# Graph network kernel: each octet's adjacency blocks leave in one store of fourteen pieces, and the two DRAM tensors are split by octet instead of by piece

## The chip, the cores and the metric

The kernel runs on one core of a Trainium2 chip. The metric is the device time of one execution in microseconds (us), the median of several runs. Lower is better.

## The reference, cut to what matters

A graph of 12,500 nodes with 96 features and 400,000 edges (sorted by destination) passes through two blocks. The first is an edge network, the second two graph convolutions that share one sparse matrix. Only the data flow matters for this change:

```python
# block 1: edge network
edge_input = concat([h[src], edge_attr])                 # 400000 x 128
messages = gelu(edge_input @ mW1 + mb1) @ mW2 + mb2
gates = sigmoid(gelu(edge_input @ gW1 + gb1) @ gW2 + gb2)
aggregated = segment_sum(messages * gates, dst)          # 12500 x 96
update = gelu(concat([h, aggregated]) @ uW1 + ub1) @ uW2 + ub2
# block 2: two layers, each
norm = dinv[row] * w * dinv[col]
xc = segment_sum(norm[:, None] * (x @ W)[row], col) + b  # the same sparse matrix in both layers
g = sigmoid(x @ Wr + br)
x = relu((1 - g) * x + g * xc)
```

## The kernel before, in words

All engines walk the edges in 196 iterations of 16 tiles (a tile is 128 edges). For each quad of four tiles GpSimd gathers the rows of the source nodes into `hid`, TensorE multiplies the edge attributes (`attr`, the product at L1099), VectorE adds the two (L1662), ScalarE applies the gelu and weighs the message (L1358), and TensorE sums the messages by destination (L1155). That is the edge network.

In 192 of the 196 iterations the engines also prepare the convolutions. About half of the edges (1,536 tiles, the "side" tiles) do not go through gathers later. They are turned into small dense adjacency blocks now: eight side tiles make an octet, one octet per iteration. TensorE builds an octet's blocks in eight parts in PSUM (`build_part`, the matmuls at L1132), and ScalarE copies each part into `blocks[h]` in SBUF (`keep_part`, L1367). `blocks` has two halves, h = 0 and 1, used by octets in turn. A full octet is 128 partitions x 98 blocks x 40 floats, 1,960 KB. SyncE's queue stores it to the DRAM tensors `adjacency` (`store_blocks`, L698). The 98 blocks are 14 pieces of seven blocks, and one piece of one octet is 280 floats, 1,120 bytes, in each partition: the longest run that is contiguous in DRAM, since the octets of a piece lie beside each other there.

The convolutions read the tensor back, once for each layer. In a layer ScalarE's queue walks 16 units of 12 octets. For a unit and a piece one load (`load_piece`, L1459) brings 128 partitions x 12 octets x 280 floats, 1,680 KB, into one of four `ring` buffers. TensorE multiplies the piece with the node table (L1240) and signals `eaten`. A piece may be loaded into a slot once the piece four earlier has been eaten. The first 14 units (seven pairs) run in a hardware loop that also carries work on the gate (`mix`), the last pair in a second one. The other half of the edges goes through gathers on GpSimd and small matmuls (L1227) between the pieces.

The order of everything is written out by hand, engine by engine, with semaphores between. What the change touches:

- `edges` on SyncE, one call per iteration. It waits for the gathers two iterations back and loads `src_ids` (L706). Then it loads `attr[0]` and `attr[1]` (L712), each once TensorE has used up that buffer's last content. The stores of the octet two iterations back are mixed in between.
- `store_blocks` waits (L563, in `wait_apart`) until ScalarE has copied all eight parts, `s_evac`.
- `keep_part` 0 of an octet waits on ScalarE until the store of the octet two earlier, which used the same half of `blocks`, has landed (`s_block_out[h]`).
- `edge_pass` builds the loop over octet pairs for every engine, and `conv_pair` and `conv_unit` on ScalarE the loop over unit pairs.

Of the kernel before, what the change touches and what calls it, by code (L numbers as in the profile page):

```python
# [30 lines left out]
P = 128  # L31
# [75 lines left out]
HALF_PIECES = PIECES // 2  # L107
# [64 lines left out]
def build(nc, io):  # L172
    ctx = contextlib.ExitStack()
    with ctx:
# [24 lines left out]
        adjacency = [dram(f"adjacency{i}", [HALF_PIECES, P, OCTETS, PIECE_Z]) for i in range(2)]  # L199
# [377 lines left out]
        def edge_pass(eng, rounds, iteration, round_end=None, part=None, round_start=None, alone=0, end=None, turns=False):  # L577

            with eng.Fori(0, rounds) as r:
                n0 = eng.snap(r * ITERS)
                o0 = eng.snap(r * OCTETS)
                w0 = eng.snap(r * OCTET_PAIRS)

                def turn(half, h):
                    return ((h, eng.snap(r * (ITERS // 2) + half)),) if turns else ()

                def prepare(c, ahead):
                    done = eng.snap(r * SLICES + c)  # L590
                    if part:
# [5 lines left out]
                def pair(w, final):  # L597
                    for h in range(2):
                        o = eng.snap(w * 2 + h) if not isinstance(w, int) else w * 2 + h
                        last = final and h == 1  # L600
                        it = o + BUILD_FROM
                        iteration(it, n0 + it, False, last, (o, eng.snap(o0 + o), h, eng.snap(w0 + w)),
                                  None if last else (o + 1, eng.snap(o0 + o + 1)), *turn(w + BUILD_FROM // 2, h))
# [12 lines left out]
                if round_end:  # L616
                    round_end(r)
# [35 lines left out]
        def _(sp):  # L653
# [40 lines left out]
            def store_blocks(o, nb, h, i):  # L694
                if i == 0:
                    wait_apart(sp, s_evac, nb * PARTS + (PARTS + EVAC_CREDIT))
                kept = blocks[h][:, :, :].rearrange("p (i c b) z -> p i c (b z)", i=2, c=HALF_PIECES)
                sp.dma_start(adjacency[i][:, :, bass.ds(o, 1), :].rearrange("c p q z -> p c (q z)"),  # L698
                             kept[:, i, :, :]).then_inc(s_block_out[h], 16)

            def edges(it, n, first, last, build, ahead, turn):
# [7 lines left out]
                for b in range(GROUPS_PER_ITER):  # L709
# [22 lines left out]
            def edges_end(r):  # L732
                o0 = sp.snap(r * OCTETS)
                for h in range(2):
                    for i in range(2):
                        store_blocks(OCTETS - 2 + h, o0 + (OCTETS - 2 + h), h, i)
                for h in range(2):
                    wait_apart(sp, s_block_out[h], r * (32 * OCTET_PAIRS) + (32 * OCTET_PAIRS + 32))
# [5 lines left out]
            for h in range(2):  # L744
                sp.sem_inc(s_block_out[h], 32)
            edge_pass(sp, rounds, edges, edges_end, round_start=edges_start, alone=1,
                      part=load_side_edges, end=keep_side_rel, turns=True)
# [547 lines left out]
        def _(act):  # L1295
# [76 lines left out]
            def edges(it, n, first, last, build, ahead):  # L1372
# [4 lines left out]
                for s in range(QUADS_PER_ITER):  # L1377
                    weigh(n, s)
                    if build:
                        keep_part(2 * s, *build[1:])  # L1380
# [8 lines left out]
                    if build:  # L1389
                        keep_part(2 * s + 1, *build[1:])  # L1390
# [54 lines left out]
            for l in range(2):  # L1445

                act.wait_ge(tb[l]["scaled"], 2 * CHUNKS)
                if l == 0:
                    for h in range(2):
                        act.wait_ge(s_block_out[h], rounds * (32 * OCTET_PAIRS) + 32)  # L1450
# [5 lines left out]
                def load_piece(w, i, u, nu, s=cv[l]):  # L1456
# [3 lines left out]
                                  adjacency[i // HALF_PIECES][i % HALF_PIECES, :, bass.ds(u * UNIT_OCTETS, UNIT_OCTETS), :]  # L1460
# [7 lines left out]
                def conv_unit(u, w, u0, h0, mix, more, s=cv[l]):  # L1468
                    nu = act.snap(u0 + u)
                    for i in range(RING, PIECES):  # L1470
                        load_piece(w, i, u, nu)
                        if mix and i in TANH_AFTER:
                            mix_tanh(h0 + (u * 2 + TANH_AFTER.index(i)))
                    if more:
                        for i in range(RING):
                            load_piece(w + 1, i, u + 1, nu + 1)
# [5 lines left out]
                def conv_pair(v, u0, h0, mix, more=True):  # L1482
                    for w in range(2):
                        conv_unit(act.snap(v * 2 + w), w, u0, h0, mix, more or w == 0)

                with act.Fori(0, passes) as p:
# [5 lines left out]
                    for i in range(RING):  # L1492
                        load_piece(0, i, 0, u0)
                    with act.Fori(0, MIX_UNITS // 2) as v:
                        conv_pair(v, u0, h0, True)
                    with act.Fori(UNITS // 2 - 1, UNITS // 2) as v:
                        conv_pair(v, u0, h0, False, False)
# [656 lines left out]
```

## Time and profile before

| | us |
|---|---|
| median of 3 runs | 8839.22 |
| lowest and highest run | 8838.54, 8855.53 |
| span of the profiled execution, core 0 | 10933.0 |
| TensorE busy in the profiled execution | 8192.3 |
| GpSimd busy | 6435.5 |
| VectorE busy | 4899.6 |
| ScalarE busy | 2690.1 |

The profiled execution is one execution, recorded by the hardware profiler. Its own time is taken to be its span, 10933.0 us, since the records show nothing around it. It is 2093.8 us longer than the median of the runs without the profiler, so its durations show proportions and what hides what, not the absolute time. TensorE's granted clock had a mean of 0.838 of full speed over the span. The program falls into setup and node tables (to about 300 us), the edge network (to about 5790 us), the node update (to about 6000 us), and the two convolution layers, each with its combination of the results (to the end).

### The profile page before, as it was taken

To read this page: it belongs to the slowest core of one execution; us is meant where nothing else is said; L and a number is where in the kernel's file an instruction comes from. 1 tells how busy PE (TensorE), PEld (TensorE's weight loads), DVE (VectorE), ACT (ScalarE), POOL (GpSimd) and SP (SyncE) were. 2 spreads that over 40 slices of the span, in tenths; PEclk is the share of its full clock that TensorE was granted. 3 is DMA by queue.
4 is the path that set the end of the run, shared out by engine and by line. 5 is a ranking of instruction groups with operands and counts; after the bars stand their busy time and mean duration, and the time that the engine had idled before them with its cause. 6 is when DMAs were issued, how large, how long until landed. Compare 5 with 4: busy or idle time off the path is not lost. (4 is left out here: it accounts for less than half of the span.)

```text
span 10933.0 us, 150076 instructions
## 1 busy us (share of the span) xinstructions
PE 8192.3 (75%) x42144; PEld 5220.9 (48%) x42144; DVE 4899.6 (45%) x11836; ACT 2690.1 (25%) x6600; POOL 6435.5 (59%) x6424
## 2 busy tenths in 40 slices
PE   4777777777777777777777578887777577887776
PEld 4555555555555555555555233333334333433333
DVE  7666666666666666666667122222222121222222
ACT  3444444444444444444443000000000000000000
POOL 4555555555555555555554666666664666666663
PEclk7888888888888888888887788888887688888887
DMA  4444444444444444444444456666565465666656
GB/s 147 123 138 131 136 132 136 132 135 132 135 133 135 133 135 135 134 135 133 135 132 134 155 207 220 216 218 214 208 212 198 156 215 206 224 217 210 210 207 207
DMA packets 933049, 1818.03 MB, mean 166 GB/s; under 512 B 277359, under 2 KB 745600, under 8 KB 875312
## 3 DMA queue, kind: packets, MB, share of 16 engines
q10 hardware_dynamic: 65600, 773.65, 18.6%
q1 hardware_dynamic: 615456, 578.39, 16.9%
q0 software_dynamic: 251856, 464.10, 14.8%
q8 instruction: 93, 1.52, 0.1%
q14 instruction: 44, 0.36, 0.0%
HBM read 1361.12 MB, written 454.48 MB: 166 GB/s over the span
## 5 line engine op out<-in xcount | busy, mean ns | idle before, releaser
L962 POOL DMA_INDIRECT hid<-src_table,src_ids x3127 | 3136.7, 1003 | 2510.4 <-ACT msg L1358 1590.2
L1240 PE MATMUL bd<-ring,table_sb 128*96 128x480 f32 x6272 | 2941.6, 614 | 513.3 <-issue 511.7
L1240 PEld LDWEIGHTS bd<-ring,table_sb 128*96 128x96 f32 x6272 | 1071.7, 176 | 2131.6 <-issue 2131.1
L1007 POOL DMA_INDIRECT hid<-conv_table,hid x1596 | 1561.9, 979 | 751.1 <-issue 486.2
L1155 PE MATMUL sg<-hot,msg 128*98 128x64 f32 x6272 | 831.1, 286 | 1115.9 <-ACT msg L1358 1105.2
L1132 PE MATMUL bd<-one_hot_dst,one_hot_src 128*128 128x168 bf16 (+1 forms) x10368 | 1277.0, 274 | 253.5 <-issue 252.3
L1007 POOL DMA_INDIRECT feat_in<-conv_table,hid x1056 | 1026.1, 972 | 545.2 <-issue 324.6
L1155 PEld LDWEIGHTS sg<-hot,msg 128*98 128x98 f32 x6272 | 746.8, 199 | 1252.2 <-issue 1180.0
L1972 DVE TENSOR_TENSOR acc<-acc,sg 96x64 f32 x400 | 87.2, 218 | 2450.0 <-remote 1652.7
L1132 PEld LDWEIGHTS bd<-one_hot_dst,one_hot_src 128*128 128x128 bf16 x10368 | 1007.1, 110 | 299.1 <-issue 284.3
L1367 ACT ACTIVATE blocks<-bd 128x480 f32<-128x480 f32 (+1 forms) x1152 | 658.1, 571 | 1704.7 <-PE bd L1132 811.8
L1709 DVE SCALAR_TENSOR_TENSOR one_hot_src<-iota_lo,side_now 128x384 bf16<-128x384 bf16 x1536 | 933.8, 608 | 0.0
L1358 ACT ACTIVATE msg<-hid,msg 128x96 f32<-128x96 f32 x3136 | 909.8, 363 | 52.7 <-DVE msg L1686 45.8
L1099 PE MATMUL pa<-w_attr,attr 128*128 128x384 f32 x1568 | 820.1, 660 | 57.9 <-DVE hid L1662 37.9
L1345 ACT ACTIVATE hid<-hid 128x768 f32<-128x768 f32 x784 | 656.8, 838 | 281.2 <-DVE hid L1662 230.6
L1465 ACT ACTIVATE buf_b<-pa,mix_b_half 96x448 f32<-96x448 f32 x56 | 35.3, 630 | 2768.6 <-remote 1515.8
L1007 POOL DMA_INDIRECT rows_more<-conv_table,hid x528 | 526.9, 998 | 301.6 <-issue 153.6
L1612 DVE TENSOR_TENSOR acc<-acc,sg 98x64 f32 x392 | 87.1, 222 | 1284.5 <-remote 1253.3
L1099 PE MATMUL pb<-w_attr,attr 128*128 128x384 f32 x1568 | 592.3, 501 | 7.8 <-issue 4.6
L1950 DVE TENSOR_TENSOR conv_hot<-iota_now,hid 128x512 f32<-128x512 f32 x134 | 92.6, 691 | 958.9 <-remote 517.0
L1099 PEld LDWEIGHTS pa<-w_attr,attr 128*128 128x128 f32 x1568 | 396.9, 280 | 262.6 <-issue 151.8
L1479 ACT ACTIVATE hid<-bd,side_flag 96x480 f32<-96x480 f32 x32 | 21.0, 657 | 1958.2 <-PE bd L1240 1126.1
(248 smaller groups left out, 10307.8 us busy)
## 6 DMA issues: line engine op xcount, KB each, us to landing
ring<-adjacency ACTq DMA_DIRECT2D x448, 1680.0 KB
adjacency<-blocks SPq DMA_DIRECT2D x384, 980.0 KB
attr<-in_attr SPq DMA_DIRECT2D x392, 128.0 KB
hid<-src_table,src_ids POOLq DMA_INDIRECT x3127
hid<-conv_table,hid POOLq DMA_INDIRECT x1596
feat_in<-conv_table,hid POOLq DMA_INDIRECT x1056
conv_table<-table_sb SPq DMA_DIRECT2D x28, 336.0 KB, 2.4
feat_half<-feat_keep SPq DMA_DIRECT2D x56, 168.0 KB
```

Of the source, the lines that this page charges most:

```text
L962: pool.indirect_dma_start(out=hid[s][:, t, :], out_offset=None, in_=src_rows, in_offset=bass.IndirectOffsetOnAxis(ap=src_ids[h][:, j:j + 1 ...
L1007: pool.indirect_dma_start(out=conv_g[j][slot][:, t, :], out_offset=None, in_=conv_rows[l], in_offset=bass.IndirectOffsetOnAxis(ap=conv_ids ...
L1099: last = nc.tensor.matmul(attr_ps[s % 2][:, 512 * h:512 * h + 2 * H2], attr[s // 2][:, P * (s % 2):P * (s % 2 + 1)], w_attr[:, 2 * H2 * h: ...
L1132: op = nc.tensor.matmul(out[:, :, bass.ds(places[q][t], FAN)], y_s[q][t][:, k, :], z_s[q][t][:, z0:z0 + FAN * m].rearrange("p (b d) -> p b ...
L1155: op = nc.tensor.matmul(sums[s // 2][0:ACC_ROWS, :], msg[s % 2][:, t, :], hot[s % 2][:, t, :], start=(s % 2 == 0 and t == 0), stop=(s % 2 ...
L1240: op = nc.tensor.matmul(side_ps[w].rearrange("r (o z) -> r o z", o=UNIT_OCTETS), table_sb[:, D * k:D * (k + 1)], ring[slot][:, :, OCTET_FA ...
L1345: nc.scalar.activation(flat, flat, ACT.Gelu).then_inc(s_gelu, 1)
L1358: op = nc.scalar.activation(m[:, t, 0:D], hid[s][:, t, 0:D], ACT.Copy, scale=m[:, t, GATE_ROW:GATE_ROW + 1])
L1367: nc.scalar.activation(blocks[h][:, first:first + m, WIDTH * q:WIDTH * (q + 1)], part_bank[i % BANKS][:, 0:WIDTH * m].rearrange("p (b w) - ...
L1709: v.scalar_tensor_tensor(out=y_s[q][t][:, :, :], in0=iota_lo[:, :].unsqueeze(1).to_broadcast([P, 3, P]), scalar=side_now[:, 0, QUAD * q + ...
L1950: v.tensor_tensor(conv_s[j][slot], iota_now[:, :].unsqueeze(1).to_broadcast([P, GROUP, WINDOW]), conv_rel[j][:, cols].unsqueeze(2).to_broa ...
L1972: v.tensor_tensor(window, window, sg[j][0:D, WINDOW * slot:WINDOW * (slot + 1)], ALU.add).then_inc(s["acc"], 1)
```

## The change

Before, each octet left in two stores of seven pieces, into `adjacency[0]` (pieces 0 to 6 of all 192 octets) and `adjacency[1]` (pieces 7 to 13 of all octets). The first came after the load of `attr[0]`, the second after the load of `attr[1]`. Now the two tensors are banks of octets: `adjacency[0]` holds all 14 pieces of octets 0 to 95, `adjacency[1]` those of octets 96 to 191. An octet leaves in one store of 14 pieces, behind both loads of `attr`. The distance between two partitions in DRAM falls from 192 x 1,120 = 215,040 bytes to 96 x 1,120 = 107,520 bytes, and that between two pieces halves too. The bytes, the runs of 1,120 bytes that a store writes, and the runs of 13,440 bytes that a load reads stay as they are.

Because a tensor cannot be chosen by a register, a loop body now belongs to one bank. SyncE's loop over octet pairs is cut in two (at pair 49). The two loops over unit pairs of a layer on ScalarE become four: pairs 0 to 2 in bank 0, pair 3 (which loads bank 0 and, ahead, the first pieces of bank 1), pairs 4 to 6 in bank 1, and pair 7. All other engines keep their code.

```diff
-HALF_PIECES = PIECES // 2
+BANK_OCTETS = OCTETS // 2
+BANK_PAIRS = UNITS // 4
...
-        adjacency = [dram(f"adjacency{i}", [HALF_PIECES, P, OCTETS, PIECE_Z]) for i in range(2)]
+        adjacency = [dram(f"adjacency{i}", [PIECES, P, BANK_OCTETS, PIECE_Z]) for i in range(2)]
...
-                with eng.Fori(alone, OCTET_PAIRS - 1) as w:
-                    pair(w, False)
-                pair(OCTET_PAIRS - 1, True)
+                ends = [alone, *([] if cut is None else [cut]), OCTET_PAIRS - 1]
+                for bank, (begin, stop) in enumerate(zip(ends, ends[1:])):
+                    with eng.Fori(begin, stop) as w:
+                        pair(w, False, bank)
+                pair(OCTET_PAIRS - 1, True, len(ends) - 2)
...
-            def store_blocks(o, nb, h, i):
-                if i == 0:
-                    wait_apart(sp, s_evac, nb * PARTS + (PARTS + EVAC_CREDIT))
-                kept = blocks[h][:, :, :].rearrange("p (i c b) z -> p i c (b z)", i=2, c=HALF_PIECES)
-                sp.dma_start(adjacency[i][:, :, bass.ds(o, 1), :].rearrange("c p q z -> p c (q z)"),
-                             kept[:, i, :, :]).then_inc(s_block_out[h], 16)
+            def store_blocks(o, nb, h, bank):
+                wait_apart(sp, s_evac, nb * PARTS + (PARTS + EVAC_CREDIT))
+                sp.dma_start(adjacency[bank][:, :, bass.ds(o - bank * BANK_OCTETS, 1), :].rearrange("c p q z -> p c (q z)"),
+                             blocks[h][:, :, :].rearrange("p (c b) z -> p c (b z)", c=PIECES)).then_inc(s_block_out[h], 16)
...
                     sp.dma_start(attr[b][:, :], chunk(io["attr"], it * 2 + b)).then_inc(s_attr[b], 16)
-                    if build:
-                        o, nb, h, _ = build
-                        if not (isinstance(o, int) and o < 2):
-                            store_blocks(o - 2, nb - 2, h, b)
+                if build:
+                    o, nb, h, _, bank = build
+                    if not (isinstance(o, int) and o < 2):
+                        store_blocks(o - 2, nb - 2, h, bank)
...
-                    act.wait_ge(s_block_out[h], w * 32 + 32)
+                    act.wait_ge(s_block_out[h], w * 16 + 16)
...
-                                  adjacency[i // HALF_PIECES][i % HALF_PIECES, :, bass.ds(u * UNIT_OCTETS, UNIT_OCTETS), :]
+                                  adjacency[bank][i, :, bass.ds(u * UNIT_OCTETS - bank * BANK_OCTETS, UNIT_OCTETS), :]
...
-                    with act.Fori(0, MIX_UNITS // 2) as v:
-                        conv_pair(v, u0, h0, True)
+                    with act.Fori(0, BANK_PAIRS - 1) as v:
+                        conv_pair(v, u0, h0, True, 0)
+                    with act.Fori(BANK_PAIRS - 1, BANK_PAIRS) as v:
+                        conv_pair(v, u0, h0, True, 0, next_bank=1)
+                    with act.Fori(BANK_PAIRS, MIX_UNITS // 2) as v:
+                        conv_pair(v, u0, h0, True, 1)
```

The first place is SyncE's queue in the body of the loop over octet pairs, one iteration of it, before. `attr_product` is the semaphore of TensorE's attribute products, `block_copied` is `s_evac`.

```order
L712 DMA attr<-in_attr 128x256
L561 ISA
L698 ISA [waits block_copied]
L698 DMA adjacency<-blocks 128x7x280
L711 REGISTER_ALU
L712 ISA [waits attr_product]
L712 DMA attr<-in_attr 128x256
L698 DMA adjacency<-blocks 128x7x280
```

The same place in the changed kernel:

```order
L713 DMA attr<-in_attr 128x256
L712 REGISTER_ALU
L713 ISA [waits attr_product]
L713 DMA attr<-in_attr 128x256
L562 ISA
L699 ISA [waits block_copied]
L699 DMA adjacency<-blocks 128x14x280
```

The second load of `attr` has moved ahead of the wait for ScalarE's copies, and one store of 14 pieces stands in place of two of seven.

The second place is ScalarE's program between two loops over unit pairs in a layer, where the body changes. Before, there is one such place in a layer, at the last pair:

```order
L1479 ACTIVATE hid<-bd,side_flag 96x480 [waits conv0_added,conv0_eaten]
L1494 REGISTER_ALU
L1494 COMPARE_AND_BRANCH
L1496 UNCONDITIONAL_BRANCH
L1458 ISA
L1459 DMA ring<-adjacency 128x3360 [waits conv0_eaten]
```

In the changed kernel there are three; this is the second of them, into the body of pairs 4 to 6:

```order
L1479 ACTIVATE hid<-bd,side_flag 96x480 [waits conv0_added,conv0_eaten]
L1497 REGISTER_ALU
L1497 COMPARE_AND_BRANCH
L1499 UNCONDITIONAL_BRANCH
L1499 ISA
L1459 ISA [waits conv0_eaten]
L1459 DMA ring<-adjacency 128x3360
```

Two further entries into a loop body per layer have been added, and the order of loads, waits and copies around them is as inside a loop. ScalarE's program grows from 748 rows to 1,108.

## Rows read from the trace of the kernel before

**Rows 1.** Cores: span and mean granted TensorE clock.

```profile
core 0: 10933.0 us, clock 0.838
```

**Rows 2.** Stretches: us, busy of PE, PEld, DVE, ACT, POOL, then clock, DMA share, GB/s.

```profile
3000.00:4000.00 1000.00, 757.80 (x5005) 573.13 (x5004) 628.93 (x1566) 441.54 (x1112) 557.38 (x557) 0.86 0.43 133
7000.00:8000.00 1000.00, 793.42 (x2791) 382.23 (x2791) 220.33 (x518) 13.42 (x21) 663.20 (x678) 0.86 0.61 216
```

**Rows 3.** Timeline of SyncE's queue: start, us, line, operation.

```profile
3018.06 0.40 SPq L698 DMA_DIRECT2D adjacency<-blocks  x1
3018.72 0.35 SPq L712 DMA_DIRECT2D attr<-in_attr  x1
3019.16 1.10 SPq L698 DMA_DIRECT2D adjacency<-blocks  x1
3046.53 0.40 SPq L698 DMA_DIRECT2D adjacency<-blocks  x1
```

**Rows 4.** Waits of SyncE's queue, 1000 to 5000 us: total, times, longest.

```profile
SPq L563 <- ACT blocks L1367: 1976.9, 139, 15.5
```

**Rows 5.** Stretches, half an iteration each: with the store, without; columns as rows 2.

```profile
3017.24:3031.50 14.26, 11.00 (x75) 8.18 (x72) 8.94 (x24) 6.35 (x16) 8.00 (x8) 0.88 0.65 206
3031.50:3045.70 14.20, 10.87 (x74) 8.44 (x72) 9.24 (x22) 6.37 (x16) 8.14 (x8) 0.88 0.23 65
```

**Rows 6.** DMA, 3017.24 to 3031.50 us in 40 slices (0.36 us each), and queues.

```profile
DMA  0000099999999999999999999465107202600620
GB/s 0 0 0 0 16 339 358 355 364 352 258 179 339 341 379 396 399 377 393 386 300 333 370 365 302 125 181 151 43 0 198 78 0 65 190 22 0 190 86 0
q1 hardware_dynamic: 2240, 2.15, 46.1%
q0 software_dynamic: 384, 0.79, 18.9%
```

**Rows 7.** Timeline of ScalarE: copies of parts into blocks, from two octets.

```profile
3017.24 0.59 ACT L1367 ACTIVATE blocks<-bd 128x500 f32<-128x500 f32 x1 [2.26 <-remote]
3047.30 0.55 ACT L1367 ACTIVATE blocks<-bd 128x480 f32<-128x480 f32 x1
```

**Rows 8.** Timeline of TensorE: attribute products, pb and pa in turn.

```profile
3012.75 1.48 PE L1099 MATMUL pb<-w_attr,attr 128*128 128x384 f32 x4
3036.81 1.49 PE L1099 MATMUL pa<-w_attr,attr 128*128 128x384 f32 x4
```

**Rows 9.** Timelines of GpSimd and VectorE: a quad's last gather, its use.

```profile
3023.81 1.00 POOL L962 DMA_INDIRECT hid<-src_table,src_ids  x1 [0.30 <-issue]
3034.83 0.95 DVE L1662 TENSOR_TENSOR hid<-pa,hid 128x768 f32<-128x768 f32 x1
```

**Rows 10.** Timeline of TensorE in the second layer: two pieces without a pause.

```profile
10679.69 5.83 PE L1240 MATMUL bd<-ring,table_sb 128*96 128x480 f32 x14
10686.68 5.83 PE L1240 MATMUL bd<-ring,table_sb 128*96 128x480 f32 x14
```

**Rows 11.** Stretch without a TensorE pause there; columns as rows 2.

```profile
10673.00:10700.00 27.00, 27.00 (x112) 13.78 (x110) 1.39 (x2) 0.00 (x0) 17.96 (x19) 1.00 0.76 282
```

**Rows 12.** Timeline of ScalarE's queue where the last pair's body begins.

```profile
8117.37 0.34 ACTq L1459 DMA_DIRECT2D ring<-adjacency  x1
8144.61 0.34 ACTq L1459 DMA_DIRECT2D ring<-adjacency  x1
```

**Rows 13.** The page, DMA queues of the whole span: packets, MB, share.

```profile
q10 hardware_dynamic: 65600, 773.65, 18.6%
q1 hardware_dynamic: 615456, 578.39, 16.9%
q8 instruction: 93, 1.52, 0.1%
```

More of the change, by code:

```diff
@@ L575, in gathers_back, with edge_pass @@
             pool.inc_swdge_sem(semaphores, counts, mode="sub").then_inc(s_round, 1)
-        def edge_pass(eng, rounds, iteration, round_end=None, part=None, round_start=None, alone=0, end=None, turns=False):
+        def edge_pass(eng, rounds, iteration, round_end=None, part=None, round_start=None, alone=0, end=None, turns=False, cut=None):
             with eng.Fori(0, rounds) as r:
@@ L595, in prepare, with pair @@
                         end(c, done)
-                def pair(w, final):
+                def pair(w, final, bank=None):
                     for h in range(2):
@@ L601, in pair @@
                         it = o + BUILD_FROM
-                        iteration(it, n0 + it, False, last, (o, eng.snap(o0 + o), h, eng.snap(w0 + w)),
+                        iteration(it, n0 + it, False, last, (o, eng.snap(o0 + o), h, eng.snap(w0 + w), bank),
                                   None if last else (o + 1, eng.snap(o0 + o + 1)), *turn(w + BUILD_FROM // 2, h))
@@ L734, in edges_end @@
                 for h in range(2):
-                    for i in range(2):
-                        store_blocks(OCTETS - 2 + h, o0 + (OCTETS - 2 + h), h, i)
+                    store_blocks(OCTETS - 2 + h, o0 + (OCTETS - 2 + h), h, 1)
                 for h in range(2):
-                    wait_apart(sp, s_block_out[h], r * (32 * OCTET_PAIRS) + (32 * OCTET_PAIRS + 32))
+                    wait_apart(sp, s_block_out[h], r * (16 * OCTET_PAIRS) + (16 * OCTET_PAIRS + 16))
             sp.wait_ge(s_never, 1)
@@ L744, in _ @@
             for h in range(2):
-                sp.sem_inc(s_block_out[h], 32)
+                sp.sem_inc(s_block_out[h], 16)
             edge_pass(sp, rounds, edges, edges_end, round_start=edges_start, alone=1,
-                      part=load_side_edges, end=keep_side_rel, turns=True)
+                      part=load_side_edges, end=keep_side_rel, turns=True, cut=BANK_OCTETS // 2 + 1)
             def store_table(c, l):
@@ L1389, in edges @@
                     if build:
-                        keep_part(2 * s + 1, *build[1:])
+                        keep_part(2 * s + 1, *build[1:4])
             act.wait_ge(s_added, 1)
@@ L1466, in mix_tanh, with conv_unit @@
                                          scale=0.5).then_inc(m["tanh"], 1)
-                def conv_unit(u, w, u0, h0, mix, more, s=cv[l]):
+                def conv_unit(u, w, u0, h0, mix, more, bank, next_bank, s=cv[l]):
                     nu = act.snap(u0 + u)
                     for i in range(RING, PIECES):
-                        load_piece(w, i, u, nu)
+                        load_piece(w, i, u, nu, bank)
                         if mix and i in TANH_AFTER:
@@ L1480, in conv_unit, with conv_pair @@
                                          scale=side_flag[0:D, 0:1]).then_inc(s["out"], 1)
-                def conv_pair(v, u0, h0, mix, more=True):
+                def conv_pair(v, u0, h0, mix, bank, more=True, next_bank=None):
                     for w in range(2):
-                        conv_unit(act.snap(v * 2 + w), w, u0, h0, mix, more or w == 0)
+                        conv_unit(act.snap(v * 2 + w), w, u0, h0, mix, more or w == 0, bank,
+                                  bank if w == 0 or next_bank is None else next_bank)
                 with act.Fori(0, passes) as p:
```

12 lines of the change are left out of this document (6 added, 6 removed).

## The prediction

> **What bounds the kernel now.** I first read the cores' view [rows 1]: one core, a span of 10933.0 us, against a median of 8839.22 us without the profiler. The sum below is made against 10933.0 us. Its change is carried to the median as it is, since it comes out near zero. The extra 2093.8 us of the profiled execution stay out of every term.
>
> Then the stretches [rows 2]. In the edge network TensorE is busy 758 of 1000 us, VectorE 629, GpSimd 557 and ScalarE 442, and the DMA engines 43%. No engine is full: the pace is set by the chain that hands a quad from engine to engine. In the convolutions TensorE is busy 793 of 1000 us, GpSimd 663, ScalarE 13, and the DMA engines 61%. SyncE and ScalarE, whose code changes, only issue transfers and wait there, and ScalarE's copies in the edge network keep their place.
>
> The question is therefore whether a store, a load of `attr`, a gather or a ring load comes late for someone. The timelines answer that. In SyncE's queue [rows 3] the first store of an octet is issued at 3018.06 us, the load of `attr[1]` at 3018.72, the second store at 3019.16, and the next octet's first store at 3046.53, 28.47 us after the last. Before the first store SyncE has waited for ScalarE: 1976.9 us in 139 waits, 14.2 us each [rows 4]. It has half of each iteration to spare.
>
> **The change part by part.**
>
> *Issuing.* An octet costs SyncE 0.40 + 1.10 = 1.50 us for its stores [rows 3]. With one store it is at least 0.40 us and at most those 1.50 us, as the bytes are the same. Over 192 octets that is up to 1.10 x 192 = 211 us less on SyncE. The 14.2 us of waiting per octet [rows 4] cover it, so I take 0. Without that cover the 211 us would be a gain.
>
> *The transfer.* The two stores are already one burst. In the half iteration that holds them the DMA engines are 90% busy or more from the sixth slice to the 25th, 20 slices of 0.357 us, 7.1 us, with 179 to 399 GB/s in each [rows 6]. There is no empty slice between the two. The same bytes in the same runs should take the same 7.1 us. Does the burst cost anything now? The half iteration with it took 14.26 us and the next, without it, 14.20 us [rows 5]. So the whole footprint of the burst is 0.06 x 192 = 11.5 us, and abolishing the stores altogether could give no more at this pace. I take 0, with 0 to -11.5 us as the bounds from these rows.
>
> The Trainium skill, on its page "DMA: Bandwidth & Descriptors", section "Anatomy of one DMA", prices a transfer at about 2.0 us plus its bytes over 436 GB/s, fitted for GpSimd's path. By that, as an estimate, two stores of 1.00 MB are 8.6 us and one of 2.01 MB is 6.6 us, 2.0 us less per octet or 384 us in all if it lay on the path. The trace does not agree that it can be saved here: the engines are full through the seam.
>
> *When an octet's buffer comes free.* ScalarE copies the last part at 3017.24 us for 0.59 us and SyncE stores at 3018.06. The same half of `blocks` is written again from 3047.30 us, where the next octet but one begins [rows 7]. The traffic of the burst is over at the latest with the 28th slice, at 3017.24 + 28 x 0.357 = 3027.2 us [rows 6], so 20 us are left. The new single store starts at the same wait. If its issue were wholly late by the old second issue it would land at about 3028.3 us, with 19 us left. ScalarE's wait stays at nothing. If this cover were gone, the copies would queue behind it, and TensorE's next parts behind those.
>
> *The load of `attr[1]`.* It moves ahead of the wait for the copies. It then waits only for the attribute product that ends at 3012.75 + 1.48 = 3014.23 us [rows 8], and so goes out up to 3.8 us earlier than at 3018.72 and no longer in the middle of the burst. The product that needs it begins at 3036.81 us [rows 8], about 18 us after the old issue. Being earlier gives nothing. What is queued behind the product's wait is the single store. TensorE's product is over before ScalarE's last copy (3017.83 us), so that wait does not delay the store. If it did, by up to 3 us, the 20 us above would cover it.
>
> *Gathers beside the burst.* The quad gathered in the burst issues its last gather at 3023.81 us for 1.00 us, and VectorE uses the rows at 3034.83 us [rows 9]. That leaves 10 us for landing, more than the 7.1 us of the entire burst. Reshaping the burst costs 0.
>
> *Ring loads.* Without a pause TensorE takes a piece in 6.99 us [rows 10]. In such a stretch the clock is at 1.00 of full speed (the 2.4 GHz level) and the DMA engines 76% busy [rows 11]. The loads read the same runs of 13,440 bytes, now 107,520 bytes apart. The trace has no load with that distance. Its cost is bounded from below at 0 (TensorE waits for its own work, so a faster read is not seen) and becomes visible once the traffic is 1 / 0.76 = 1.3 times as slow. [...] I take 0.
>
> *ScalarE's loops.* Two more body entries per layer, four in all. At an entry the four ring slots are already ordered. The next load may go out when the first piece has been eaten, 7 us into the unit, and its piece is wanted 28 us into it. A piece is 1.72 MB, and at the burst's 390 GB/s [rows 6] takes about 4.4 us, 5 with its landing. So 28 - 7 - 5 = 16 us of lateness are hidden. What can an entry cost? The code itself: 93 instruction packets took 0.1% of 16 engines' span [rows 13], 0.001 x 10933 x 16 / 93 = 1.9 us each, and the rounding allows 0.9 to 2.8 us. An entry needs one or two, so 2 to 6 us. The one entry the trace shows has 27.24 us between two ring loads [rows 12], but TensorE paused in it, so that is only the upper bound. I take the near end, which is hidden: 0. The far end is (27.24 - 16) x 4 = 45 us.
>
> SyncE's one more loop entry is covered by the same 14.2 us of waiting.
>
> Sum: 0 against 10933.0 us, with -11.5 and +45 us as the ends that the rows leave. I forecast 8838 us for the median, 1 us under that of before: the likeliest entries to a loop cost nothing, and the one small term left, the burst's, can only give.
>
> **The rivals.**
>
> *A gain from the seam between two stores.* If what a store costs beyond its bytes held back SyncE or the gathers at the faster pace of an unprofiled run, one store fewer could give up to 1.10 x 192 = 211 us: 8628 us. For it: the second issue really is 1.10 us, against 0.40 for the first. Against it: the full slices, the equal halves, and 14.2 us of slack. Without the profiler an iteration is shorter, by at most 2094 / 196 = 10.7 us if all of the difference lay there, and 3.5 of the 14.2 us would still be left. Chance 0.03. The skill's formula above is the same case and would give 8455 us.
>
> *The closer layout is read or written faster.* Both tensors' rows lie half as far apart, and an octet's store touches one tensor instead of two. If the ring loads do sometimes hold TensorE in an unprofiled run, 1% of the 448 pieces' 6.99 us is 31 us: 8808 us. Against it: 24% of idle DMA time at full pace. Chance 0.06.
>
> *Slower: ScalarE enters a new body late.* Place: the four added entries. If the code arrives more than 16 us after the branch, the fifth piece of the unit is late and TensorE waits. At the full 27.24 us the price is 45 us: 8884 us. Against it: 1.9 us per packet, and ScalarE is busy 13 of 1000 us there [rows 2]. The Trainium skill, page "Runtime: NRT & Kernel Launch", section "Instruction fetch mechanics", says that a taken branch whose target is outside the two pages held must fetch before it goes on. That speaks against adding bodies. The trace shows instruction packets, but none that cost 16 us. Chance 0.06.
>
> *Slower: memory likes the new distance less.* From 1.3 times the traffic time on, each further percent costs 31 us; at 1.33 times it would be 8932 us. Or the one long burst holds gathers back beyond their 10 us: each 0.1 us in an iteration is 19 us. Chance 0.05 together.
>
> *No change that can be measured*: 0.80.
>
> **How the numbers follow.** A measurement of this kernel can tell about 0.2%, 18 us, from no change (the three runs differ by 17 us). The likeliest case has 0.80, and its own range is 8822 to 8857 us. Faster by over 0.2% has 0.03 + 0.06, rounded to 0.09. Slower has 0.06 + 0.05 = 0.11. The range reaches a little into both sides, for the first percent of a better layout and the first microseconds of a late entry: 8812 to 8866 us.
>
> **What would show it right or wrong.** In SyncE's timeline an octet should show two loads of `attr` with the second 3 to 5 us before the store, then one store of 1960 KB with 0.4 to 1.5 us of issue. The DMA slices should again be full for about 7 us. The halves of an iteration should stay at 14.2 to 14.3 us with and without the burst. ScalarE's first copy of an octet should have no wait on a DMA. In the convolutions the stretch with full clock should again take 6.99 us per piece at about 76% DMA share. The prediction fails if a half with the burst grows by more than 0.1 us over a half without, if the share of DMA in a stretch without pauses leaves 0.70 to 0.85, or if TensorE waits for `ring` after an added loop entry.

## The result, and the profile after

| | before | after |
|---|---|---|
| median, us (4 runs each, side by side) | 8841.09 | 8919.45 |
| lowest, highest | 8838.54, 8855.53 | 8903.36, 8928.08 |
| ratio, 95% interval | 1 | 1.0079 [1.0067, 1.0091] |

The changed kernel is slower by 0.79%, about 70 us by the ratio (the two medians of four lie 78 us apart). Its profiled execution has a span of 8901.5 us, close to its median. That is the first surprise, since the profiled execution of before took 10933.0 us [rows 1]. So the unchanged kernel was profiled again in the first experiment. The cores' view of that second profile:

```profile
core 0: 8858.0 us, clock 0.918
```

The same view of the changed kernel:

```profile
core 0: 8901.5 us, clock 0.916
```

An execution like the one behind [rows 1 to 13] is not what the medians time: it was longer by nearly a quarter and had a clock of 0.838. From here on the second profile of before stands for before. The two normal spans differ by 43.5 us, of the about 70 in the medians.

Where the 43.5 us are, the tiles' view tells. Its rows give the count, the duration in ns (least, median, most), the first and last start in us. First the stores and the ring loads, before:

```profile
L698 SPq DMA_DIRECT2D adjacency<-blocks x384: 372/488/1274, 301.6 to 4417.1; - x192
L1459 ACTq DMA_DIRECT2D ring<-adjacency x448: 334/339/643, 4635.7 to 8737.0; - x150
```

The same of the changed kernel:

```profile
L699 SPq DMA_DIRECT2D adjacency<-blocks x192: 372/407/412, 298.9 to 4463.3; - x192
L1459 ACTq DMA_DIRECT2D ring<-adjacency x448: 333/339/602, 4681.3 to 8782.4; - x150
```

The ring loads take 4101.3 us from the first to the last before and 4101.1 us after. The convolutions, with the new layout and four more loop entries, did not change. From the first to the last store it is 4115.5 us before and 4164.4 after: all of the loss is in the edge network.

What paces it there is seen in stretches (columns as in [rows 2]). Before:

```profile
1000.00:4000.00 3000.00, 2614.44 (x20045) 2009.65 (x20044) 2536.67 (x6269) 1790.37 (x4456) 2317.40 (x2230) 0.96 0.59 179
```

After:

```profile
1000.00:4000.00 3000.00, 2603.15 (x19785) 1999.28 (x19785) 2500.43 (x6190) 1764.64 (x4399) 2312.01 (x2201) 0.95 0.58 177
```

GpSimd issues 16 gathers in an iteration, so an iteration is 3000 / 2230 x 16 = 21.52 us before and 3000 / 2201 x 16 = 21.81 us after. Over 192 iterations the 0.28 us between them are 54 us, near the 48.9 us by which the stores' stretch grew. Waits in the same stretch (us in total, times, longest), before:

```profile
POOL hid L962 <- issue: 632.2, 2066, 1.2
POOL hid L962 <- ACT msg L1358: 50.6, 164, 1.0
DVE hid L1662 <- DMA hid<-src_table,src_ids: 371.4, 151, 3.7
```

After:

```profile
POOL hid L962 <- issue: 649.9, 2091, 2.0
POOL hid L962 <- ACT msg L1358: 38.4, 110, 2.0
DVE hid L1667 <- DMA hid<-src_table,src_ids: 394.4, 138, 4.5
```

GpSimd stands 2317.40 + 632.2 + 50.6 = 3000 us of 3000 in gathers and in the pauses around them, and a pause is 0.31 us in the mean: it hardly ever waits for anybody. Its gathers set the pace. An iteration's 0.28 us are 16 x (2312.01 / 2201 - 2317.40 / 2230) = 0.18 us of longer gathers (1.050 us each for 1.039) and 0.10 us of longer pauses. And VectorE does wait for a gather, about once per octet: 371.4 / 151 = 2.46 us before, 394.4 / 138 = 2.86 us after.

In the first profile of before the same rows were otherwise:

```profile
POOL hid L962 <- ACT msg L1358: 857.6, 251, 4.2
POOL hid L962 <- issue: 469.6, 1419, 2.1
```

There GpSimd waited for ScalarE to be done with a buffer, 857.6 / 251 = 3.4 us each time, and the 10 us between a gather and its use [rows 9] were the slack of that slower pace.

SyncE's timeline (start, us, line, operation), an octet of before:

```profile
2005.34 0.40 SPq L698 DMA_DIRECT2D adjacency<-blocks  x1
2005.98 0.35 SPq L712 DMA_DIRECT2D attr<-in_attr  x1
2006.43 1.17 SPq L698 DMA_DIRECT2D adjacency<-blocks  x1
2014.93 0.37 SPq L706 DMA_DIRECT2D src_ids<-in_src  x1
2026.47 0.40 SPq L698 DMA_DIRECT2D adjacency<-blocks  x1
```

An octet of the changed kernel:

```profile
2011.38 10.01 SPq L713 DMA_DIRECT2D attr<-in_attr  x2
2021.83 0.41 SPq L699 DMA_DIRECT2D adjacency<-blocks  x1
2030.31 0.38 SPq L707 DMA_DIRECT2D src_ids<-in_src  x1
2043.26 0.41 SPq L699 DMA_DIRECT2D adjacency<-blocks  x1
```

The last copy of a part, from ScalarE's timeline of the changed kernel:

```profile
2019.75 0.57 ACT L1367 ACTIVATE blocks<-bd 128x500 f32<-128x500 f32 x1
```

And the product on which `attr[1]` waits, from its timeline of TensorE:

```profile
2019.32 1.55 PE L1099 MATMUL pb<-w_attr,attr 128*128 128x384 f32 x4
```

The copy ends at 2020.32 us, but the product at 2020.87, and only then come the load and the store, at 2021.83. In the octet of before the last copy began at 2004.53 us and took 0.57, so its store went out 0.24 us after it. Over all octets from 1000 to 4000 us the first store follows the end of the last copy by 0.24 us before and by 1.60 us after. At the slower pace of the first profile the product had ended before the copy [rows 7, 8].

### The profile page after: what moved, and what is told of

The parts are those of the page before. It is cut to its first block, busy times and chain, and to the rows that moved or that the text cites. A ratio compares the mean times of both kernels' runs of the same rounds, so it can differ in the third digit from the quotient of the medians.

```text
span 8901.5 us, 149729 instructions
## 1 busy us (share of the span) xinstructions
PE 7416.7 (83%) x42144; PEld 4785.5 (54%) x42144; DVE 4925.9 (55%) x11836; ACT 2716.2 (31%) x6600; POOL 6553.3 (74%) x6424
## 4 chain that ended last, share of the span: by engine, by line
POOL 48%; issue 24%; DMA 10%; DVE 7%; PE 7%; ACT 2%; DVEq 1%; POOLq 1%; SPq 0%; ACTq 0%
POOL hid L962 17%; POOL hid L1007 14%; POOL feat_in L1007 11%; DMA hid<-src_table,src_ids 6%; POOL rows_more L1007 5%; DMA hid<-in_src 1%; DVE hid L1667 1%; DVE one_hot_src L1714 1%; PE bd L1132 1%; PE pb L1099 1%; ACT msg L1358 1%; DMA rows_more<-conv_table,hid 1%; PE sg L1155 1%; PE pa L1099 1%; POOLq L562 1%
## 5 line engine op out<-in xcount | busy, mean ns | idle before, releaser
L962 POOL DMA_INDIRECT hid<-src_table,src_ids x3127 | 3281.4, 1049 | 1040.8 <-issue 928.5
L1240 PE MATMUL bd<-ring,table_sb 128*96 128x480 f32 x6272 | 2708.7, 587 | 0.0
L1132 PE MATMUL bd<-one_hot_dst,one_hot_src 128*128 128x168 bf16 (+1 forms) x10368 | 1150.5, 266 | 0.0
L1099 PE MATMUL pb<-w_attr,attr 128*128 128x384 f32 x1568 | 707.4, 581 | 485.1 <-DVE hid L1667 484.7
L1155 PE MATMUL sg<-hot,msg 128*98 128x64 f32 x6272 | 682.2, 254 | 61.4 <-ACT msg L1358 61.4
L1099 PE MATMUL pa<-w_attr,attr 128*128 128x384 f32 x1568 | 610.7, 513 | 105.6 <-DVE hid L1667 84.1
L1155 PEld LDWEIGHTS sg<-hot,msg 128*98 128x98 f32 x6272 | 640.9, 174 | 73.2 <-DVE acc L1617 47.8
L1667 DVE TENSOR_TENSOR hid<-pb,hid 128x768 f32<-128x768 f32 x392 | 373.5, 953 | 550.7 <-DMA hid<-src_table,src_ids 550.4
L1099 PEld LDWEIGHTS pb<-w_attr,attr 128*128 128x128 f32 x1568 | 299.1, 212 | 670.7 <-DVE hid L1667 531.7
L1713 DVE TENSOR_SCALAR one_hot_dst<-iota_z,side_now 128x688 bf16<-128x688 f16 x1152 | 509.3, 442 | 0.0
```

Of the source, the lines that this page charges most:

```text
L962: pool.indirect_dma_start(out=hid[s][:, t, :], out_offset=None, in_=src_rows, in_offset=bass.IndirectOffsetOnAxis(ap=src_ids[h][:, j:j + 1 ...
L1099: last = nc.tensor.matmul(attr_ps[s % 2][:, 512 * h:512 * h + 2 * H2], attr[s // 2][:, P * (s % 2):P * (s % 2 + 1)], w_attr[:, 2 * H2 * h: ...
L1132: op = nc.tensor.matmul(out[:, :, bass.ds(places[q][t], FAN)], y_s[q][t][:, k, :], z_s[q][t][:, z0:z0 + FAN * m].rearrange("p (b d) -> p b ...
L1155: op = nc.tensor.matmul(sums[s // 2][0:ACC_ROWS, :], msg[s % 2][:, t, :], hot[s % 2][:, t, :], start=(s % 2 == 0 and t == 0), stop=(s % 2 ...
L1240: op = nc.tensor.matmul(side_ps[w].rearrange("r (o z) -> r o z", o=UNIT_OCTETS), table_sb[:, D * k:D * (k + 1)], ring[slot][:, :, OCTET_FA ...
L1667: v.tensor_tensor(pair, attr_ps[s % 2][:, :].rearrange("p (b c) -> p b c", b=2)[:, :, 0:2 * H2], pair, ALU.add).then_inc(s_added, 1)
```

## The experiments

Each kernel was timed side by side with before. "Iteration" is 3000 us over the number of gathers from 1000 to 4000 us, times 16, from the stretches' row of each; "start" is the mean time from the end of an octet's last copy to its first store in the same stretch, worked out from the timelines, with the least and the most where they are far apart. The ratio of the unchanged kernel to itself was 1.000 [0.9991, 1.001].

| kernel | what | start, us | iteration, us | ratio [95%] |
|---|---|---|---|---|
| before | two stores, attr[1] between | 0.24 | 21.52 | 1 |
| after | one store behind attr[1] | 1.60 | 21.81 | 1.0079 [1.0067, 1.0091] |
| e2 | two stores behind attr[1] | 1.61 | 21.81 | 1.0068 [1.0055, 1.0082] |
| e3 | layout and loops, two stores at old places | 0.24 | 21.51 | 1.0001 [0.9992, 1.001] |
| e4 | one store ahead of attr[1] | 0.24 | 21.53 | 1.0008 [0.9999, 1.0018] |
| e5 | before, first store waits for the product | 1.03 | 21.64 | 1.0036 [1.0022, 1.005] |
| e6 | first half after part 5 | -5.4 (-7.7 to -3.8) | 21.63 | 1.0025 [1.0014, 1.0036] |
| e15 | first half after part 6 | -2.1 | 21.62 | 1.0014 [1.0005, 1.0023] |
| e9 | stores one part later | 2.62 | 21.72 | 1.0057 [1.0044, 1.0071] |
| e10 | stores two parts later | 5.2 | 21.57 | 1.0017 [1.0007, 1.0026] |
| e7 | stores behind the next `src_ids` | 5.6 (3.0 to 9.2) | 21.68 | 1.0048 [1.0034, 1.0062] |
| e8 | half the bytes, old place | 0.24 | 21.60 | 1.0004 [0.9995, 1.0013] |
| e14 | half the bytes, behind attr[1] | 1.21 | 21.43 | 0.9972 [0.9962, 0.9983] |
| e12 | 1/14 of the bytes, old place | 0.24 | 21.44 | 0.9977 [0.9967, 0.9986] |
| e13 | 1/14 of the bytes, behind attr[1] | 1.20 | 21.44 | 0.9974 [0.9963, 0.9985] |
| e11 | VectorE without `one_hot_src` | 0.24 | 20.84 | 0.9864 [0.9849, 0.9879] |

**The parts of the change, one at a time.** e1 is before unchanged.

> The kernel before, unchanged, for a second profiled execution. The profile of the changed kernel has a span of 8901.5 us, close to its median, while that of before had 10933.0 us. If the long span was an accident of that one execution, this profile has a span of about 8840 us, an iteration of the edge network of about 22 us instead of 28.5, and GpSimd as the engine that is busy most of it. If profiling this kernel costs 2000 us by itself, the span is near 10900 us again. The time against before is 1.000 either way.

e2 takes the order alone, in the kernel before:

```diff
                     sp.dma_start(attr[b][:, :], chunk(io["attr"], it * 2 + b)).then_inc(s_attr[b], 16)
-                    if build: ... store_blocks(o - 2, nb - 2, h, b)
+                if build: ... for i in range(2): store_blocks(o - 2, nb - 2, h, i)
```

> The kernel before with one edit: both stores of seven pieces are issued behind both loads of attr; tensors, piece halves and loops are those of before. Theory A (order): the store now waits on SyncE behind the wait for the attribute product, starts about 1 us later and meets other gathers, and VectorE waits for a gather beside each store: about +0.8%, near 8910 us. Theory B (one store of 14 pieces holds the DMA rings against the gathers longer than two stores with a load between them): about 8840 us. Theory C (the closer distance of rows in DRAM): about 8840 us. Theory D (ScalarE's added loop bodies in the convolutions): about 8840 us.

e3 is the changed kernel (banks and cut loops) with two stores at the old places, e4 the changed kernel with its one store ahead of `attr[1]`:

```diff
-                if build:
+                    if build and b == 0:
```

> The changed kernel with two stores of seven pieces at the old two places; the tensors are banks of octets, and the loops are cut as in the changed kernel. Theory A: about 8840 us. Theory B: about 8840 us. Theory C: about 8919 us, with the store's burst or the ring loads longer than before. Theory D: about 8919 us, with the difference in the two convolution layers and none before them.

> The changed kernel with its single store of 14 pieces at the place of the old first store, between the load of attr[0] and that of attr[1]. Theory A (the wait for the attribute product delays the store): about 8840 us. Theory B (the single long store itself): about 8919 us or more, as attr[1] now stands behind all of the store. Theories C and D: about 8919 us.

e2 has the whole loss and e3 and e4 none of it (e4's interval just touches 1). So neither the layout, nor the added loop entries, nor the merging of two stores costs or gives anything; the order of `attr[1]` and the store does it.

**Late store, or early load?** e5 keeps the order of before and only makes the first store wait for the same product:

```diff
+                            if b == 0:
+                                sp.wait_ge(s_attr_mm, QUADS_PER_ITER * (n - 1) + 4)
                             store_blocks(o - 2, nb - 2, h, b)
```

> The kernel before with one wait added: SyncE waits for the attribute product (the wait of the second load of attr) already ahead of the first store; the order of loads and stores stays store, load of attr[1], store. Runs so far: both stores behind the load of attr[1] gave 1.0068 and started 1.6 us after ScalarE's last copy, where before they start 0.2 us after it. Theory A1 (the delay of the first store by that wait is the cause): about +0.7%, near 8915 us. Theory A2 (the cause is that the load of attr[1] is ahead of the stores rather than between them): no change, about 8855 us.

It costs 0.36% at a start of 1.03 us, half of the loss at about half of the delay. The wait in front of the store is what costs. Here the gathers alone carry it: 16 of them take 16 x 2321.93 / 2218 = 16.75 us for 16.63 in before, which is all of the iteration's 0.12 us. If later is worse, is earlier better? e6 lets the first seven pieces leave two parts earlier, when those that hold them are copied (both stores stand ahead of `attr[1]` here):

```diff
-                if i == 0:
-                    wait_apart(sp, s_evac, nb * PARTS + (PARTS + EVAC_CREDIT))
+                wait_apart(sp, s_evac, nb * PARTS + ((6, PARTS)[i] + EVAC_CREDIT))
```

> The kernel before with the first store (pieces 0 to 6, blocks 0 to 48) issued as soon as part 5 of an octet's eight is copied, some 4 us before the last part; the second store as before behind part 7, and the load of attr[1] behind both. Theory A1 in its simple form (the earlier an octet's traffic starts, the less it holds back the gathers that VectorE waits for, 0.28 us per octet for 1.4 us): faster by 0.3 to 1%, 8770 to 8830 us. Theory A3 (it is the place of the burst among the gathers that counts, and before's is simply a good one): anywhere, no faster or slower, with VectorE waiting for other gathers.

e7 holds both stores back until the next `src_ids` has been loaded:

```diff
                              ).then_inc(s_ids[h], 16)
+                if build: ... for i in range(2): store_blocks(o - 3, nb - 3, 1 - h, i)
                 for b in range(GROUPS_PER_ITER):
...
-                    if build: ... store_blocks(o - 2, nb - 2, h, b)
```

> The kernel before with both stores of an octet some 9 us later, behind the load of the next iteration's src_ids and ahead of its attr[0]. The buffer is wanted again only some 21 us after the old place, so the landing itself (about 7 us) is still hidden. Theory A1 in its simple form (later is worse): slower than 1.007, perhaps by 1.5% or more. Theory A3 (place among the gathers): not ordered by lateness; it may be as fast as before or faster, since it meets the gathers of the other half of the iteration.

Both are slower than before, so the loss is not "the later the worse". The stores of e7 do not start some 9 us after the last copy, as its expectation and the later ones have it, but at 3.0 to 9.2 us, 5.6 in the mean, since the loads of `src_ids`, behind which they stand, come earlier than in before. (The first store of e6 is likewise 5.4 us early in the mean, in two groups of about 4 and 7 us, not the 4 us of the expectations.) e7's loss is also of another kind. Its gathers take what they take in before (2300.33 / 2214 = 1.039 us), and the pauses between them are longer, 0.316 us for 0.306, with more waits for ScalarE (90.5 us in 241).

**How it depends on the start.** e9 and e10 keep before's order and wait for one or two of ScalarE's parts more (`+ 1`, `+ 2`); e15 is e6 one part later, with `(7, PARTS)`.

```diff
-                    wait_apart(sp, s_evac, nb * PARTS + (PARTS + EVAC_CREDIT))
+                    wait_apart(sp, s_evac, nb * PARTS + (PARTS + EVAC_CREDIT + 1))
```

> The kernel before with the wait of an octet's first store set one part later: it waits until part 0 of the next octet is copied too, about 2 us after the last part of its own. Order and number of loads and stores as before. Runs so far, as start of the first store behind the last copy: 0.23 us gives 1.000, 1.03 us (wait for the attribute product alone) 1.0036, 1.6 us (both stores behind the load of attr[1]) 1.0068, about 9 us 1.0048, and the first half 4 us earlier 1.0025. Theory A1 (delay near the old place costs, whatever causes it, and the order against attr[1] does not matter): 1.006 to 1.010, 8910 to 8940 us. Theory A2 (part of the cost of the changed kernel comes from attr[1] being ahead of both stores): no more than 1.004, 8890 us.

> The same with the wait two parts later, about 4 us after the last copy. If the cost keeps growing with the delay: above 1.01, over 8940 us. If it is the place of the burst between the gathers that counts, the curve bends back towards the 1.0048 that 9 us gave: 1.000 to 1.008.

> All traffic, the first store of seven pieces issued when part 6 of eight is copied, about 2 us ahead of the last; second store behind part 7, attr[1] behind both. Points so far, first store against the last copy: about 4 us earlier 1.0025, 0.2 us later 1.000, 1.0 us 1.0036, 1.6 us 1.0068, 2.6 us 1.0057, about 5 us 1.0017, about 9 us 1.0048. A smooth curve through them puts this one at 0.999 to 1.002. If earlier than before is better at first, it is below 0.998 and beats both kernels.

e9 has the order of before and 0.57%: the order of store and `attr[1]` as such is not the cause. The loss is largest for starts of 1.6 and 2.6 us after the copy and small again at 5.2. But the mean start alone does not set it, since e7 with 5.6 us loses 0.48% and e10 with 5.2 us 0.17%. No start that was tried is better than that of before. The burst does not cost by being late for its reader: in the changed kernel ScalarE's copies wait for no store. That it costs by what it meets is what remains, and is not shown directly.

VectorE's wait for gathers does not tell a slow version from a fast one. Per iteration it is 2.66 us in before and 2.87 in the changed kernel, but 2.53 in e9 (348.8 us of 3000, with 0.57% lost) and 1.69 in e10 (234.5 us, with 0.17% lost).

**The burst's bytes.** e8 leaves the second store out, and the convolutions read pieces 0 to 6 in place of 7 to 13. e12 and e13 store piece 0 alone and read it for all; e14 is e8 with its store behind `attr[1]`.

```diff
+                if i:
+                    return
-                sp.dma_start(adjacency[i][:, :, bass.ds(o, 1), :]...
+                sp.dma_start(adjacency[i][0:1, :, bass.ds(o, 1), :]...   # e12, e13
...
-                             kept[:, i, :, :]).then_inc(s_block_out[h], 16)
+                             kept[:, i, :, :]).then_inc(s_block_out[h], 32)
```

> The kernel before without the second store of each octet: pieces 7 to 13 are not stored, and the convolutions read pieces 0 to 6 in their place (the same load traffic, wrong values for half of the blocks). It prices the burst. If the store's traffic delays gathers on VectorE's path at all: faster by 0.5 to 2% (VectorE's wait beside the store, 2.6 us, should shrink by half or vanish; at most 1.3 x 192 = 250 us). If the burst's footprint is the 11.5 us that was read from the first profile: no change within 0.2%.

> The kernel before storing only piece 0 of the 14 of each octet, at the old place of the first store; the convolutions read piece 0 in place of all (same load traffic in bytes, wrong values). It leaves 1/14 of the store's traffic. Theory T (the burst's traffic delays gathers and so costs time even at its old place): faster than before, 0.98 to 0.995. Theory L (only the way in which gathers, VectorE and GpSimd fall into step counts, and at the old place the burst costs nothing): within 0.3% of before, as the half store was (1.0004).

> The same single piece, but stored behind both loads of attr, as the changed kernel does. If the traffic is what acts in the changed kernel (theories T and L alike), it makes no difference to the run with one piece at the old place, within 0.2%. If something else does, such as SyncE's own waits or the load of attr[1] ahead of the store, it is 0.5 to 0.8% slower than that run.

> Half of each octet (pieces 0 to 6) stored behind both loads of attr; the convolutions read pieces 0 to 6 twice. At the old place half the traffic gave 1.0004. If the traffic acts and its amount counts: between 1.000 and 1.005. If only the start counts: 1.006 to 1.008. If nothing of the traffic matters at the late place: as the one piece behind.

With 1/14 of the bytes the two orders are equal (0.9977 and 0.9974), so the waits in SyncE's queue cost nothing by themselves. With half of the bytes the late place is no worse either (0.9972 for 1.0004). That points to the burst's traffic. The stretch and VectorE's wait in e12:

```profile
1000.00:4000.00 3000.00, 2565.63 (x20138) 1953.65 (x20137) 2593.88 (x6296) 1803.26 (x4479) 2318.16 (x2239) 1.00 0.35 93
```

```profile
DVE hid L1664 <- DMA hid<-src_table,src_ids: 322.1, 416, 2.0
```

Without the burst VectorE waits for gathers too, but 0.8 us at a time and three times per iteration, not 2.5 to 2.9 us once. From e12 to before the time grows by 1 - 0.9977 = 0.23%; at the late place, from e13's 0.9974 to e2's 1.0068 or the changed kernel's 1.0079, about 1.0%.

These differences are not the price of the bytes alone. The granted clock was 1.00 in e12, e13 and e14 from 1000 to 4000 us, and 0.95 or 0.96 in every version with the whole burst and in e8. e8 and e14 store the same bytes, and the one with the clock at 1.00 is faster by 0.32%, though its store is the later. So the clock, or what goes with it, can be worth as much as the 0.23%. Whether the late place would cost anything with the whole burst at a clock of 1.00 was not tested. Among the versions with the whole burst the clock does not order the times: e5 has 0.96 as before and is slower by 0.36%, e10 has 0.95 as the changed kernel and loses 0.17%.

**GpSimd as the pace.** In before a gather takes 0.95 us, except beside some of VectorE's operations. Timeline of GpSimd, before:

```profile
2000.09 0.95 POOL L962 DMA_INDIRECT hid<-src_table,src_ids  x1 [0.30 <-issue]
2001.34 1.77 POOL L962 DMA_INDIRECT hid<-src_table,src_ids  x1 [0.30 <-issue]
2003.42 0.95 POOL L962 DMA_INDIRECT hid<-src_table,src_ids  x1 [0.30 <-issue]
```

Timeline of VectorE over the second of them:

```profile
2001.22 0.61 DVE L1709 SCALAR_TENSOR_TENSOR one_hot_src<-iota_lo,side_now 128x384 bf16<-128x384 bf16 x1
2001.75 0.55 DVE L1671 TENSOR_TENSOR prod<-hid,gate_w 128x384 f32<-128x384 f32 x1
2002.33 0.55 DVE L1674 TENSOR_REDUCE buf_h<-prod 128x4 f32<-128x384 f32 x1
```

e11 takes the first of these operations away: `one_hot_src` is built once, before the first octet, and not again, so that all later octets use the first one's.

```diff
+                    if spread:
+                        for k in range(2):
+                            v.scalar_tensor_tensor(out=y_s[k][t][:, :, :], ...)
...
-                    v.scalar_tensor_tensor(out=y_s[q][t][:, :, :], ...).then_inc(s_yz, 1)
+                    op.then_inc(s_yz, 1)
```

> The kernel before without VectorE's L1709 (one_hot_src, 0.61 us, eight times an octet) except once before the first octet: the adjacency blocks are built from a stale factor, everything else is done. GpSimd is busy 77% with gathers and 21% between them in the edge network, and its gathers take 0.94 us at best and 1.04 us on average. Theory G (GpSimd's gathers set the pace, and run longer where VectorE works beside them): the mean gather falls below 1.00 us, and the iteration of 21.5 us shortens by about 16 x the fall, 0.6 to 1.5 us, 8570 to 8740 us. If GpSimd's pace does not depend on VectorE and VectorE's own chain is not the bound: no change, 8855 us. If VectorE's chain is the bound: up to 8 x 0.61 = 4.9 us an iteration, down to 7900 us.

```profile
1000.00:4000.00 3000.00, 2659.34 (x20734) 2079.39 (x20732) 2004.90 (x5320) 1812.03 (x4607) 2297.12 (x2303) 0.96 0.60 185
```

A gather falls from 1.039 to 2297.12 / 2303 = 0.997 us and an iteration from 21.52 to 20.84 us. Of these 0.68 us the shorter gathers are 16 x 0.042 = 0.67; the pauses stay as they are. VectorE was not the bound in before: it is busy 2536.67 us of 3000, and in e11, with less to do, it waits for gathers 724.3 us instead of 371.4. Yet 1.36% come back, through the gathers beside it.

Sorting the 2,230 gathers of before by what VectorE does during them says the same. The 218 with nothing beside them take 0.945 us in the mean and 0.96 at most. The 975 beside `one_hot_src` take 1.146 us. The 1,030 beside neither `one_hot_src` nor `prod` take 0.950.

## Why the prediction was wrong

- **What bounds the kernel now** was the step that failed first. "No engine is full: the pace is set by the chain that hands a quad from engine to engine" was true of the profiled execution of 10933.0 us, not of those that the median times. There GpSimd is at its gathers without a break. "The extra 2093.8 us of the profiled execution stay out of every term" did not keep them out: each slack (14.2 us of SyncE's waiting [rows 4], halves of 14.26 and 14.20 us [rows 5], 10 us for a gather [rows 9]) belongs to that slower pace. The rival on the seam did shorten an iteration, by up to 10.7 us, but took it from SyncE's 14.2 us alone. Taken from the gather's 10 us as well, it would have left nothing.
- **The load of `attr[1]`.** "TensorE's product is over before ScalarE's last copy (3017.83 us), so that wait does not delay the store" was read rightly from [rows 7, 8] and does not hold at the normal pace, where the product ends 0.55 us after the copy. The fallback, "if it did, by up to 3 us, the 20 us above would cover it", priced the delay against the wrong reader. The 20 us cover the half of `blocks`, and ScalarE indeed waits for no store. The delay of 1.4 us shows in the gathers. (A small slip stands beside it: from 3014.23 to 3018.72 us are 4.5 us, not 3.8.)
- **Gathers beside the burst.** "Reshaping the burst costs 0" failed as a term of the sum: the merge itself is free (e4), but the burst in its new place cost 0.28 us per iteration in longer gathers and pauses, 54 us. The rival with "each 0.1 us in an iteration is 19 us" had the right place (the gathers) and price, and the wrong trigger (a longer burst; it was a later one) and too small a chance.
- **Issuing, the seam, the layout, ring loads, ScalarE's loops**, all taken at 0: right. e3 gives 1.0001, e4 1.0008, and the ring loads keep their 4101 us. The cover named for them was still too large: at the normal pace SyncE waits 1145.2 us in 139 waits for the copies, 8.2 us each, not 14.2.
- **What the trace should show.** The store did come right behind the second load and not 3 to 5 us after it, which alone says that the order of product and copy had been the other way round.

What is shown: the order alone makes the loss (e2), a wait ahead of the store alone makes half of it (e5), it is gone with half of the bytes or fewer (e13, e14; at a clock of 1.00), and it lies in the time of the gathers and the pauses between them. What is only argued: that the burst at that time delays a gather's landing, that VectorE's operations then come closer together, and that they lengthen the following gathers. The trace gives no landing times for the gathers, and VectorE's waits do not follow the loss. Why a start of 5.2 us is nearly harmless and 1.6 to 2.6 us is not, why e7 loses by its pauses, and what the clock adds, stays open. None of the versions that do all the work beats before.

## What to carry to other kernels

Compare the span of a profiled execution with the median before reading any slack from it; if they are far apart, its waits and idle times belong to another execution. When an instruction moves behind a wait in a queue, ask at the true pace which of the two conditions comes last, and price the delay against the engine that sets the pace and its transfers, not only against the one who needs the buffer. With a tuned order, move one instruction at a time: the merge here was free and the move that came with it cost 0.7%.

## What was unexpected of the hardware

A gather instruction's time on GpSimd depends on VectorE: 0.94 to 0.96 us alone, up to 1.8 us beside it, 1.039 us in the mean, and 0.997 us with eight of VectorE's operations per octet (`one_hot_src`) gone. The Trainium skill, page "SBUF — State Buffer", section "SBUF: two separate sides", says that the two engines share a pair of ports, which VectorE holds for a whole instruction in some modes or with two operands in SBUF (the latter only against a GpSimd operation that reads SBUF), and that a VectorE operation in such a mode keeps GpSimd from writing the descriptors of a DMA. The trace agrees in kind. The gather of 1.77 us lies over two operations with two operands in SBUF, `one_hot_src` and `prod`. The 100 gathers of before with only L1662 beside them, one of whose operands lies in PSUM, take 0.945 us, as those with nothing beside them. But the 146 beside L1662 and L1682 take 0.946, though L1682 too reads two operands in SBUF, so the runs do not settle which operations count.

The time also does not follow the start of a burst in one direction: 1.0000 at 0.24 us, 1.0068 at 1.6, 1.0057 at 2.6, 1.0017 at 5.2, and 1.0048 where the start lies between 3.0 and 9.2.
